# Layer norm rows applied on another engine, and q and k stacked by head triples

## The reference

```
x = x + moe_a(group_norm(x))      # 8 experts, top 2, 96 -> 384 -> 96, gelu
t = t + attention(layer_norm(t))  # 6 heads of 16, causal, 1024 tokens
t = t + moe_c(layer_norm(t))      # 4 experts, top 2, 96 -> 384 -> 96, gelu
layer_norm(v) = (v - mean(v)) / sqrt(var(v) + eps)      # over the 96 channels of a token
attention: softmax(q k^T / sqrt(16), causal) v, then a projection
```

## Time and profile before

| | |
|---|---|
| time of the profiled execution | 1521.14 us |
| its span, first to last instruction | 1519.3 us |
| mean granted TensorE clock | 0.913 |
| TensorE busy | 1309.2 us (86%) |
| VectorE busy | 904.2 us (60%) |
| ScalarE busy | 946.4 us (62%) |
| GpSimd busy | 785.3 us (52%) |

### The profile page before, as it was taken

One profiled execution on the slowest core, in us unless ns is written; L12 is line 12 of the kernel. 1 busy time (PEld: TensorE's weight loads), 2 busy tenths in 40 slices (PEclk: granted clock), 3 DMA queues, 4 the chain that ended last, 5 costly groups with the idle time before them and its releaser, 6 DMA issues.

```text
span 1519.3 us, 32843 instructions
## 1 busy us (share of the span) xinstructions
PE 1309.2 (86%) x12573; PEld 757.5 (50%) x12573; DVE 904.2 (60%) x2662; ACT 946.4 (62%) x1880; POOL 785.3 (52%) x782
## 2 busy tenths in 40 slices
PE   4788878889898899898998898988998898968877
PEld 1554542466535564365635565365643666232355
DVE  4866583378717784287734777167852876165353
ACT  2566547566685567656686666755677566704745
POOL 4775541557536474366725575364744566201546
PEclk9897998999999899999999899998999999956988
DMA  5000200400031000400003000310003000120100
GB/s 110 12 2 15 50 1 12 75 2 2 13 60 26 2 2 23 74 2 2 3 22 75 2 2 13 62 25 1 2 23 65 1 2 2 39 47 1 24 12 12
DMA packets 37390, 34.76 MB, mean 23 GB/s; under 512 B 26091, under 2 KB 28012, under 8 KB 37234
## 3 DMA queue, kind: packets, MB, share of 16 engines
q1 hardware_dynamic: 20594, 26.37, 9.0%
q10 hardware_dynamic: 16640, 6.29, 1.6%
HBM read 22.62 MB, written 9.63 MB: 21 GB/s over the span
## 4 chain that ended last, share of the span: by engine, by line
PE 55%; DVE 23%; DMA 7%; issue 4%; DVEq 3%; ACT 3%; POOL 3%; SPq 2%; POOLq 0%; ACTq 0%
PE ps_y L636 20%; PE ps_u L636 18%; PE ps_r L636 9%; PE ps_m L636 6%; DVE mpart L1156 5%; DVE xn L1138 4%; DMA qk_dram<-qk_l 3%; DVE acc L1097 3%; DMA ks<-qk_dram 3%; POOL hidl L615 2%; DVE yt L1288 2%; PE ps_m L655 1%; ACT hidh L928 1%; DVEq L1140 1%; SPq L505 1%
## 5 line engine op out<-in xcount | busy, mean ns | idle before, releaser
L615 POOL TENSOR_TENSOR hidl<-hid,hidh 128x512 f16<-128x512 f32 x576 | 673.5, 1184 | 389.8 <-ACT hidh L928 383.9
L927 ACT ACTIVATE hid<-ps_u 128x512 f32<-128x512 f32 x576 | 344.2, 598 | 402.3 <-PE ps_u L636 373.9
L636 PEld LDWEIGHTS ps_y<-w2s,hidh 128*128 128x128 f16 x4608 | 289.7, 101 | 166.3 <-issue 38.5
L1156 DVE TENSOR_REDUCE mpart<-ps_r 128x1 f32<-128x512 f32 (+2 forms) x576 | 297.3, 549 | 102.1 <-PE ps_r L636 91.0
L636 PE MATMUL ps_y<-w2s,hidh 128*128 128x96 f16 x4608 | 336.5, 212 | 7.2 <-DVE acc L1097 7.2
L928 ACT ACTIVATE hidh<-ps_u 128x512 f16<-128x512 f32 x576 | 341.2, 592 | 0.0
L636 PE MATMUL ps_r<-ks,qs 96*128 96x512 f16 (+2 forms) x576 | 203.6, 369 | 88.6 <-DVE mpart L1156 51.5
L636 PE MATMUL ps_y<-w2s,hidl 128*128 128x96 f16 x2304 | 233.2, 212 | 4.8 <-POOL hidl L615 3.9
L587 POOL TENSOR_SCALAR_AFFINE_SELECT probs<-probs 128x384 f32<-128x384 f32 x128 | 66.7, 523 | 306.5 <-ACT probs L959 306.4
L636 PE MATMUL ps_u<-xah,w1h 97*128 97x512 f16 x408 | 169.8, 416 | 22.2 <-ACT hidh L928 17.3
L959 ACT ACTIVATE probs<-ps_r 128x512 f32<-128x512 f32 (+3 forms) x352 | 152.2, 506 | 45.1 <-PE ps_r L636 45.0
(11 more groups left out here) (183 smaller groups left out, 1487.3 us busy)
## 6 DMA issues: line engine op xcount, KB each, us to landing
rb<-rsum_dram SPq DMA_DIRECT2D x24, 256.0 KB, 4.3
qs<-qk_dram SPq DMA_DIRECT2D x24, 192.0 KB, 4.7
ks<-qk_dram SPq DMA_DIRECT2D x24, 192.0 KB, 4.9
xin<-in_x_dram ACTq DMA_DIRECT2D x8, 384.0 KB, 4.3
qk_dram<-qk_h SPq DMA_DIRECT2D x16, 192.0 KB, 2.9
qk_dram<-qk_l SPq DMA_DIRECT2D x16, 192.0 KB, 3.5
out_dram<-xo ACTq DMA_DIRECT2D x8, 384.0 KB, 2.9
w_raw<-in_L_conv_W_dram SPq DMA_DIRECT2D x8, 288.0 KB, 5.0
```

The source lines that it names most:

```text
L615: g.tensor_tensor(hidl[:, grp.k % HB, j, :], hid[:, j, :], hidh[:, grp.k % HB, j, :], ALU.subtract).then_inc(hl_ready, 1)
L636: return nc.tensor.matmul(dst, lhsT, rhs, start=start, stop=stop, skip_group_check=True)
L927: a.activation(hid[:, j, :], bank[:], ACT.Gelu, scale=1.0 / WS)
L1156: v.tensor_reduce(mpart[:, h, i, part:part + 1], ps_r[k % 3][:, 0:w], AX, ALU.max).then_inc(mx_free, 1)
```

## The change

1. `ln_apply` moves from VectorE to ScalarE. GpSimd now makes a second row of numbers per token, `shift` = -mean * rstd, by one multiplication before and one after the power, and ScalarE computes Identity(rstd * x + shift) with both numbers per partition. The slots of the chores stay.
2. The loads of `qs` and `ks` are cut by heads. Both writes to device memory are issued as soon as q and k are there (`keep_qk`); the loads for heads 0 to 2 (6 DMAs) need only that the first half of the score matmuls is done, and those for heads 3 to 5 (6 DMAs) that all are. The first maximum waits for the first set, the 37th for the second.
3. The maxima of phase A are spread over slots 3 to 63 in place of 8 to 63.
4. The multiplication by -1/256 goes into the split after the transpose.
5. `x2_turn`, `logits_c`, `exp_c`, `route_c` unit 3 and `x_turn` move by one to three slots.

```diff
-TO_C = [(27, "ln2_apply", 0), (28, "ln2_apply", 1), (30, "x2_turn", 0), (32, "x2_turn", 1), (34, "logits_c", 0),
-        (36, "exp_c", 0)]
-ROUTE_C = [(38, "route_c", 0), (40, "route_c", 1), (42, "route_c", 2), (44, "route_c", 3), (48, "gates_c", 0)]
+TO_C = [(27, "ln2_apply", 0), (28, "ln2_apply", 1), (31, "x2_turn", 0), (33, "x2_turn", 1), (35, "logits_c", 0),
+        (37, "exp_c", 0)]
+ROUTE_C = [(38, "route_c", 0), (40, "route_c", 1), (42, "route_c", 2), (45, "route_c", 3), (48, "gates_c", 0)]
-GN = [(37, "x_turn", 0), (39, "x_turn", 1), (54, "gn_stats", 0), ...
+GN = [(39, "x_turn", 0), (42, "x_turn", 1), (54, "gn_stats", 0), ...
-                   *maxima_at(8, SLOTS_A - 1, 0, MAX_A)),
+                   *maxima_at(3, SLOTS_A - 1, 0, MAX_A)),
...
-            def stack_qk(s, b):
+            def keep_qk(s, b):
                 wait(sp, qk_split, b.value(2, s + 1))
                 for n, part in enumerate((qk_h, qk_l)):
                     sp.dma_start(qk_dram[n, s], part[:, s, :]).then_inc(qk_out, 16)
-                if s == 0:
-                    wait(sp, s_full, b.value(SU, 0))
-                wait(sp, qk_out, b.value(64, 32 * (s + 1)))
-                dst, parts = ((qs, (0, 1, 0)), (ks, (0, 0, 1)))[s]
-                for n, part in enumerate(parts):
-                    sp.dma_start(dst[HD * n:HD * (n + 1), :, :],
-                                 qk_dram[part, s].rearrange("(h d) t -> d h t", h=H)).then_inc(qk_stacked, 16)
+
+            def stack_qk(t, b):
+                wait(sp, s_full, b.value(SU, (t - 1) * half))
+                wait(sp, qk_out, b.value(64, 64))
+                heads = slice(TR * t, TR * (t + 1))
+                for s, (dst, parts) in enumerate(((qs, (0, 1, 0)), (ks, (0, 0, 1)))):
+                    for n, part in enumerate(parts):
+                        sp.dma_start(dst[HD * n:HD * (n + 1), heads, :],
+                                     qk_dram[part, s, heads.start * HD:heads.stop * HD, :]
+                                     .rearrange("(h d) t -> d h t", h=TR)).then_inc(qk_stacked[t], 16)
...
                 if name == "qk" and k % NC == NC - 1:
-                    stack_qk(k // NC, b)
+                    keep_qk(k // NC, b)
+                    if k // NC == 1:
+                        for t in range(2):
+                            stack_qk(t, b)
...
+            def rstd_shift(dst, shift, mv, ready, done, b):          # GpSimd
+                pool.wait_ge(ready, b.value(1, 1))
+                g.tensor_tensor(shift, mv[:, :, 0], minus[:], ALU.mult)
+                g.tensor_tensor(dst, mv[:, :, 1], epsilon[:], ALU.add)
+                pool.drain()
+                g.tensor_tensor(dst, dst, power[:], ALU.pow)
+                pool.drain()
+                g.tensor_tensor(shift, shift, dst, ALU.mult).then_inc(done, 1)
...
-                    pe.wait_ge(qk_stacked, b.value(16 * QK_DMAS, 16 * QK_DMAS))
+                    pe.wait_ge(qk_stacked[0], b.value(16 * QK_DMAS, 16 * QK_DMAS))
                     wait(pe, p_ready, b.value(SU, 0))
+                if k == MAXU // 2:
+                    pe.wait_ge(qk_stacked[1], b.value(16 * QK_DMAS, 16 * QK_DMAS))
...
+            def ln_apply(dst, src, rstd, shift, got, ready, b, half):          # ScalarE
+                if half == 0:
+                    act.wait_ge(got, b.value(1, 1))
+                for t in range(TC * half, TC * (half + 1)):
+                    last = a.activation(dst[:, t, :], src[:, t, :], ACT.Identity, bias=shift[:, t:t + 1],
+                                        scale=rstd[:, t:t + 1])
+                last.then_inc(ready, 1)
...
-                v.tensor_scalar(used, used, -1.0 / MS, None, ALU.mult).then_inc(mneg_ready, 1)
...
-                split(mth[:], mtl[:], ps_m[0:H * TT, 0:P], 1.0).then_inc(m_free, 1)
+                split(mth[:], mtl[:], ps_m[0:H * TT, 0:P], -1.0 / MS).then_inc(m_free, 1)
```

More of the change, by code:

```diff
@@ L352, in build @@
         rstd2 = sb("rstd2", [P, TT])
+        shift1 = sb("shift1", [P, TT])
+        shift2 = sb("shift2", [P, TT])
+        minus = sb("minus", [P, TT])
         xn1 = sb("xn1", [P, TT, D])
@@ L359, in build @@
         mpart = sb("mpart", [P, H, TT, 2])
-        mneg = sb("mneg", [P, P])
+        mtop = sb("mtop", [P, P])
         mth = sb("mth", [H * TT, P], F16)
@@ L436, in build @@
         acc_ready = sem("acc_ready")
-        qk_split, qk_out, qk_stacked = sem("qk_split"), sem("qk_out"), sem("qk_stacked")
+        qk_split, qk_out = sem("qk_split"), sem("qk_out")
+        qk_stacked = [sem(f"qk_stacked{t}") for t in range(2)]
         v_ready = sem("v_ready")
         hi_ready = sem("hi_ready")
-        mneg_ready, m_split, m_stacked = sem("mneg_ready"), sem("m_split"), sem("m_stacked")
+        mtop_ready, m_split, m_stacked = sem("mtop_ready"), sem("m_split"), sem("m_stacked")
         yt_ready, sums_in, rsum_ready = sem("yt_ready"), sem("sums_in"), sem("rsum_ready")
@@ L446, in build @@
         QK_DMAS = 2 * 3
+        half = SU // 2
         x_d = x.rearrange("b (t q) w c -> b (q w) t c", t=TT)
@@ L558, in _ @@
             g.iota(expert[:], pattern=[[0, TT], [1, 8]], base=0, channel_multiplier=0)
-            for tile, value in ((epsilon, 1e-5), (power, -0.5), (ra.gates, 0.0), (rc_.gates, 0.0),
+            for tile, value in ((epsilon, 1e-5), (power, -0.5), (minus, -1.0), (ra.gates, 0.0), (rc_.gates, 0.0),
                                 (rc_.prob, -1.0), (b2a, 0.0), (b2c, 0.0), (wpad, 0.0)):
@@ L562, in _ @@
             pool.drain()
-            for tile, value in ((identb, 0.0), (mask_q, 0.0), (mpart, NEG), (mneg, 0.0)):
+            for tile, value in ((identb, 0.0), (mask_q, 0.0), (mpart, NEG), (mtop, 0.0)):
                 g.memset(tile[:], value)
@@ L601, in chore @@
                 if name == "ln1" and k == 1:
-                    rstd(rstd1[:], mv1[:, :, 1], ln1_var, ln1_rstd, b)
+                    rstd_shift(rstd1[:], shift1[:], mv1, ln1_var, ln1_rstd, b)
                 if name == "ln2" and k == 1:
-                    rstd(rstd2[:], mv2[:, :, 1], ln2_var, ln2_rstd, b)
+                    rstd_shift(rstd2[:], shift2[:], mv2, ln2_var, ln2_rstd, b)
             grp = Count()
@@ L785, in maxima_turn @@
             def maxima_turn(b):
-                pe.wait_ge(mneg_ready, b.value(1, 1))
+                pe.wait_ge(mtop_ready, b.value(1, 1))
                 shared()
-                nc.tensor.transpose(ps_m[:, 0:P], mneg[:], ident[:]).then_inc(m_full, 1)
+                nc.tensor.transpose(ps_m[:, 0:P], mtop[:], ident[:]).then_inc(m_full, 1)
             def soft_scores(b, n):
@@ L983, in chore @@
                                  ).then_inc(hi_ready, 1)
+                if name == "ln1_apply":
+                    ln_apply(xn1, x1, rstd1, shift1, ln1_rstd, xn1_ready, b, k)
+                if name == "ln2_apply":
+                    ln_apply(xn2, x2, rstd2, shift2, ln2_rstd, xn2_ready, b, k)
                 if name == "exp_a":
@@ L1132, in ln_stats @@
                     dve.drain().then_inc(ready, 1)
[L1134 to L1140, removed]
             def split_qk(s, c, b):
@@ L1160, in maxima @@
                 dve.drain()
-                used = mneg[:, 0:H * TT]
-                v.tensor_reduce(used.rearrange("p (h i) -> p h i", h=H), mpart[:], AX, ALU.max)
-                dve.drain()
-                v.tensor_scalar(used, used, -1.0 / MS, None, ALU.mult).then_inc(mneg_ready, 1)
+                used = mtop[:, 0:H * TT]
+                v.tensor_reduce(used.rearrange("p (h i) -> p h i", h=H), mpart[:], AX, ALU.max).then_inc(mtop_ready, 1)
                 wait(dve, m_stacked, b.value(32, 0))
                 shared()
-                split(mth[:], mtl[:], ps_m[0:H * TT, 0:P], 1.0).then_inc(m_free, 1)
+                split(mth[:], mtl[:], ps_m[0:H * TT, 0:P], -1.0 / MS).then_inc(m_free, 1)
                 dve.drain().then_inc(m_split, 1)
```

6 lines of the change are left out of this document (1 added, 5 removed).

## The result

The changed kernel takes 1400.95 us (median of 4 runs, 1397.22 to 1401.64) where the kernel before takes 1519.61 beside it: a ratio of 0.9215, 95% interval 0.9171 to 0.9259. The gain is 119 us. Most of the difference, 34 us, is one term, the clock.

A forecast was written before the change was run, and what follows sets the result against it. TensorE was taken as the bound, losing 86.6 us to waits and 63 us to the clock. Terms 12.7 + 24.2 + 8.8 + 3.1 + 21 + 11 = 80.8 us off 1521.1 gave 1440 us, range 1414 to 1484.

The forecast's parts named there:

- clock: Six images: TensorE's mean clock of 0.94 loses 63 us; between bounds 0 and 42, 21 us taken as regained.
- loads of q and k: Phase A, six images: the 19.9 us wait for `ks` goes, 1.2 us per image stays; 12.7 us gained.
- layer norm rows, net: Six images: waits behind layer norms go, 18.6 and 14.6 us, less 6 and 3 on ScalarE; net 24.2 us.
- small moves and scaling: Six images: the 8.8 us wait for `xt` goes, and 3.1 us of the 6.2 for scaled maxima.
- other iterations: Outside the six images: iteration 8 moves forward by 10 us, with small changes elsewhere; sum 11 us.
- Rival 3: Six images: the clock comes back whole, 21 us more, 1419 us; chance 0.12.
- the fourth maximum behind `sum_inverse`: Phase A, slot 7: it needs the first maximum reduced, which VectorE does after inverting the sums; a wait of 1.2 us.
- Rival 2: Phase A: the sums take the place of `ks`, so the loads' gain falls to nothing; 1458 us, chance 0.15.
- my signs of being wrong: Fourth maximum waiting 3 us on VectorE; TensorE waiting for Gelu behind slots 27 and 28 or 10 and 11; clock still 0.94.
- Rival 1: Layer norms: ScalarE gives the gain back, at 34 us in place of 9; 1479 us, chance 0.16.
- rival 4: Layer norms on ScalarE: Identity needs a table other than Gelu's, 5.1 us of loads each; slower, 1541 us, chance 0.03.
- Its wait stays: `route_c` unit 3, one slot later with the same work on VectorE: its wait of about 2.8 us per image stays.

The follow-up runs named there:

- e2: Changed kernel with q and k loads as before (all heads at once) and maxima from slot 8 again: 1444.74 us, ratio 0.9521 to the kernel before.
- e1: Changed kernel with the layer norm rows applied on VectorE again: 1446.80 us, ratio 0.9540 to the kernel before.
- e3: Changed kernel with `x2_turn`, `exp_c`, `route_c` unit 3 and `x_turn` back in their old slots: 1422.80 us, ratio 0.9364 to the kernel before.
- made waits: Changed kernel with TensorE made to wait in phase A for small unused DMAs from SyncE; five versions, 1398.93 to 1457.95 us.
- the repeats: Changed kernel measured again without edits, twice: 1399.40 and 1401.51 us.
- e9: Changed kernel with `route_c` unit 3 alone back in slot 44: 1406.67 us, ratio 0.9263 to the kernel before.
- e17: Changed kernel with layer norm halves apart, maxima from slot 8 and `gates_c` in slot 50: 1397.04 us, ratio 0.9211 to the kernel before.
- e11: Changed kernel with TensorE waiting for two small DMAs in a row at one place per image: 1408.14 us, ratio 0.9269 to the kernel before.
- e13: Changed kernel with TensorE waiting for three small DMAs in a row at one place per image: 1423.07 us, ratio 0.9377 to the kernel before.
- e14: Changed kernel with TensorE waiting for three small DMAs in a row at four places per image: 1457.95 us, ratio 0.9634 to the kernel before.
- e15: Changed kernel unchanged, measured again beside other runs: 1399.40 us, ratio 0.9230 to the kernel before.
- e18: Changed kernel unchanged, measured again beside the version with layer norm halves apart: 1401.51 us, ratio 0.9245 to the kernel before.
- e10: Changed kernel with TensorE asking for one small DMA at one place per image: 1400.25 us, ratio 0.9224 to the kernel before.
- e12: Changed kernel with TensorE asking for one small DMA at each of four places per image: 1398.93 us, ratio 0.9229 to the kernel before.

## Why the prediction was wrong in size, step by step

| term | predicted us | measured us | from |
|---|---|---|---|
| loads of q and k | 12.7 | 18.1 | idle time of e2 less that of after |
| layer norm rows, net | 24.2 | 25.5 | idle time of e1 less that of after |
| small moves and scaling | 11.9 | 18.7 | idle time of e3 less that of after (the scaling is not in it) |
| all waits | 48.8 | 56.2 | idle time, before less after |
| clock | 21 | 54.8 | busy time, before less after |
| other iterations | 11 | 8.3 | outside the six images |

The first three rows overlap: measured one by one they are 62.3 us, together 56.2.

**The step that failed is the clock's.** "Two thirds of the 63 us would be 42 ... bounds 0 and 42, taken 21". It divided the lost clock in proportion to the microseconds of wait and then halved it, for fear that what stays keeps the clock down. Both halves of that were wrong. The made waits show that a wait's clock price is not in proportion to its length: those of 1.1 to 1.4 us brought no fall, and those of 2.2 to 2.4 us one each, 2.1 us of clock on average. Taking single parts back shows that each kind of long wait brings falls of its own (21.9, 14.7 and 8.4 us of busy time, 45 of the 54.8). The change left no long wait but one of up to 2.1 us for `gatesc`, and with the many short ones the clock stays at 1.00, or falls once for 3.4 us in the repeats. So the upper bound of 42 was itself too low. Rival 3, the clock whole at 1419, had the right event and the wrong size, as it also took 42 for the whole.

**Loads of q and k.** Right: no maximum waits for a DMA. What I expected to be late next, the fourth maximum behind `sum_inverse` with 1.2 us, did not wait. VectorE inverts 6.8 us into phase A (438.77 against 431.99), where it was 13.4 before; the 5.8 us that I forecast came as 6.6. Rival 2 did not happen: the loads of 96 KB landed in 3.0 us (`qs`) and 3.9 us (`ks`) at the median, and those behind them were not held back: the sums are inverted 1.6 us after their last issue (437.21 to 438.77), where before it was 2.5. The estimate of 6 us for three more transfers rests on the fixed cost of about 2 us that the Trainium skill gives (DMA: Bandwidth & Descriptors, "Anatomy of one DMA — SWDGE (gpsimd) path"). The page measured it for DMAs issued by GpSimd, and these are issued by SyncE; 6 us are not seen on the path here. The first set was issued by 424.9 and lands in 3.9, and is wanted at 436.35.

**Layer norm rows.** The net is right to 1.3 us, and its parts nearly. Against e1, the waits for maxima fall from 38.2 to 2.9 us, 35.3 gained (predicted 18.6 + 14.6 = 33.2), and the waits for Gelu rise from 16.3 to 27.3, 11 lost (predicted 9). One size inside was wrong without harm. The group of these instructions after (count | busy us, mean ns | idle before):

```profile
L966 ACT ACTIVATE xn<-x,shift,rstd 128x96 f32<-128x96 f32 x128 | 48.5, 457 | 21.7 <-POOL shift L618 21.7
L618 POOL TENSOR_TENSOR shift<-shift,rstd 128x8 f32<-128x8 f32 x16 | 3.2, 202 | 2.3
```

An Identity takes 457 ns, above the 290 of the earlier trace rows that I had as its upper bound, and eight take 3.0 to 3.1 us in place of 1.4. The Trainium skill (ScalarE: Activation LUTs, "Rules for kernel authors") budgets about 0.3 us for an activation plus 0.83 ns for each element, which is 3.0 us for eight of 96, an estimate; this trace agrees with it, and not with my 1.4. The step is still cheap: in phase A two groups of four delay a Gelu by 1.5 us each, and in phase C one group of eight by 3.0 us, of which 1.0 and 1.4 us reach TensorE, and no fall stands behind them. TensorE waiting for Gelu behind these slots was among my signs of being wrong, and it came, at about the size that I had priced. Rival 1, in which ScalarE gives it back at 34 us, did not happen. Nor did rival 4: no table load stands beside an Identity.

**Small moves.** The copies of `xt` no longer hold TensorE (8.8 us), and the scaling brought 3.8 us (6.2 to 2.4) for a forecast of 3.1. "Its wait stays", said of `route_c` unit 3, was wrong: it was the largest wait that I had left in, and e9 shows that the move of one slot took it away (with the neighbouring chores moved back as well, in e3, it is longer). In e9 that wait alone costs only 7.4 us in the six images, so it explains little of the 33.8 us of clock that I missed. It was not argued from rows whether maxima would queue behind a chore one slot later, and that could have been done.

**Cancelling errors.** Gelu waits cost 17.0 us more than before (10.3 to 27.3), 11 of them by the layer norm and the rest by other parts; I had 9. The `route_c` wait, whose loss I had not predicted (11.2 us by e9), more than covers the 8 us of difference. That the waits together came within 7.4 us of the forecast is in part luck.

**What stays open.** Why some long waits bring no fall (2.80 us in e9) and some short ones do, and what sets whether a fall lasts 3.4 or 6.8 us. The kernel before has 119.6 us at half clock and the three taken-back parts 98.6 together; no run shows where the other 21 us belong. The scaling of the maxima was not taken back alone.

## What to carry to other kernels

Price a wait of the bound engine by its length: here made waits up to 1.4 us cost about themselves, and one of 2.3 us in a busy stretch nearly twice itself, so take away the long waits first and let a few short ones come in their place. Count the clock as an effect of the long waits, not as a share of all waits, and ask whether any long one is left; here almost none was, and nearly the whole loss of the six images came back. A small elementwise step on an engine that shares time with a busy neighbour can be moved to one that is slower per instruction and still gain, as long as the queue behind it catches up. When the waits are down to this size, read busy time as well as idle time: in e17 two thirds of the idle time that was won went back to the clock.

## What the runs showed of the hardware

- A made wait of 1.17 us in a busy stretch left the granted clock at 1.00; one of 2.33 us brought 0.50 for 6.8 us. Of the made waits of e11, e13 and e14, none of the eleven of 1.1 to 1.8 us brought a fall, all six of 2.2 to 2.4 us in e13 did, and 13 of the 17 of 2.0 to 2.3 us in e14. Length alone does not decide: the changed kernel has single waits of 1.7 us (Gelu) and 2.1 us (`gatesc`) and no time at 0.50 in its six images, while in e15 the first and in e18 the second brought a fall of 3.4 us; in e9 three of five waits of 1.75 us brought one.
- Identity with a scale and a bias per partition, 128x96 float32, takes 457 ns on ScalarE, four in a row 1.54 us and eight 2.97 us, with no table load beside Gelu.
- On VectorE a 128x32 or 128x64 operation with two tensors beside GpSimd's unbroken `hidl` takes 1.1 to 1.2 us, in the last rows of the timeline after. Where GpSimd is idle the same two instructions take 0.22 and 0.19 us (at 1294.55 and 1294.85 in the same trace). The Trainium skill (SBUF, State Buffer, "Who interferes with whom") says that a VectorE instruction with two inputs in SBUF contends with a GpSimd instruction that reads SBUF; this trace agrees.
- Strided loads of 96 KB, six in a row, landed 3.0 us (`qs`) and 3.9 us (`ks`) after issue at the median.
- A signal sent by TensorE's queue runs ahead of its matmuls: one small DMA, asked for and waited for at once, made no matmul wait (e10, e12). In e11 SyncE issues the first DMA at 337.0, 1.2 us before the matmuls ahead of the made wait have ended (339.60 less 1.40).
